# LayerNorm normalisations on VectorE: one scalar_tensor_tensor with a broadcast 1/std in place of tensor_scalar

## What is computed

```python
def _layernorm(x, axis=-1, eps=1e-05):
    m = jnp.mean(x, axis=axis, keepdims=True)
    v = jnp.var(x, axis=axis, keepdims=True)
    return (x - m) / jnp.sqrt(v + eps)

x = x + tanh(g_xattn[0]) * attn0(_layernorm(x), ctx)    # 16 heads of 64
x = x + tanh(g_ffn[0])   * moe0(_layernorm(x))          # 8 experts, thresholded softmax gate
x = x + tanh(g_xattn[1]) * attn1(_layernorm(x), ctx)    # 16 heads of 16
x = x + tanh(g_ffn[1])   * moe1(_layernorm(x))          # routed experts, first 512 rows only
```

## Time and profile before

| | |
|---|---|
| median of 3 runs | 3775.74 us (3772.87 to 3776.51) |
| the profiled execution, its own time | 3774.71 us |
| its span, first to last instruction | 3772.6 us |
| TensorE clock granted, mean | 0.996 of full |
| TensorE busy | 3665.2 us, 97% |
| VectorE busy | 2636.4 us, 70% |
| ScalarE busy | 1711.5 us, 45% |
| GpSimd busy | 1386.7 us, 37% |

### The profile page before, as it was taken

How to read it: one execution, slowest core, us unless ns; L and a number is a source line. 1 busy time by engine, 2 the same in 40 slices (tenths; PEclk the granted TensorE clock), 3 DMA queues, 4 the chain that set the end, 5 groups by cost and what they waited for, 6 DMA issues and landing times.

```text
span 3772.6 us, 95482 instructions
## 1 busy us (share of the span) xinstructions
PE 3665.2 (97%) x34836; PEld 2991.3 (79%) x34836; DVE 2636.4 (70%) x5694; ACT 1711.5 (45%) x3115; POOL 1386.7 (37%) x1333
## 2 busy tenths in 40 slices
PE   7999999999999999999999999999999999999998
PEld 5778878878878878878878878878878878878865
DVE  4676776776776776776776776776776776776775
ACT  4444444444444444444444444444444444444431
POOL 3333433433433433433433433433433433433323
PEclk9999999999999999999999999999999999999999
DMA  3000000000000000000000000000000000000001
GB/s 96 11 14 16 12 12 16 12 12 16 12 12 16 12 12 16 12 13 16 12 13 16 11 13 16 12 13 16 12 13 16 11 13 16 11 13 16 11 26 65
DMA packets 58916, 64.83 MB, mean 17 GB/s; under 512 B 5344, under 2 KB 55808, under 8 KB 58240
## 3 DMA queue, kind: packets, MB, share of 16 engines
q10 hardware_dynamic: 34688, 32.52, 2.8%
q1 hardware_dynamic: 24192, 31.81, 2.6%
HBM read 47.01 MB, written 17.30 MB: 17 GB/s over the span
## 4 chain that ended last, share of the span: by engine, by line
PE 91%; DVE 6%; ACT 1%; issue 1%; POOL 0%; SPq 0%; DMA 0%; DVEq 0%; ACTq 0%; POOLq 0%
PE g L818 28%; PE g L824 17%; PE scores L818 12%; PE scores L921 6%; PE g L971 6%; DVE xn L1177 4%; PE g L887 4%; PE g L990 3%; PE scores L955 3%; PE scores L981 3%; PE g L838 3%; PE scores L925 2%; PE g L898 1%; DVE kT_lo L1207 1%; ACT kT_hi L663 1%
## 5 line engine op out<-in xcount | busy, mean ns | idle before, releaser
L761 ACT ACTIVATE prob<-scores 120x1024 f32<-120x1024 f32 x512 | 498.5, 1023 | 509.0 <-PE scores L925 438.4
L1316 DVE SCALAR_TENSOR_TENSOR x<-g,lg_w,x 128x256 f32<-128x256 f32 x1024 | 494.8, 483 | 250.3 <-PE g L818 226.7
L597 POOL TENSOR_TENSOR q_lo<-an,q_hi 128x512 fp32r<-128x512 f32 x256 | 331.7, 1308 | 278.0 <-ACT q_hi L790 278.0
L818 PE MATMUL g<-ew_hi,yT_hi 128*128 128x512 f32 x1024 | 426.5, 416 | 0.0
L818 PE MATMUL g<-ew_lo,yT_hi 128*128 128x512 f32 x1024 | 401.7, 392 | 0.0
L818 PE MATMUL g<-ew_hi,yT_lo 128*128 128x512 f32 x1024 | 399.5, 390 | 0.0
L1255 DVE TENSOR_REDUCE y_nm<-g 128x4 f32<-128x480 f32 x512 | 301.0, 650 | 110.6 <-PE g L898 110.6
L542 POOL TENSOR_TENSOR y_rstd<-y_mv,eps 128x2 f32<-128x2 f32 x128 | 25.0, 195 | 960.7 <-DVE y_mv L1172 960.7
L1255 DVE TENSOR_REDUCE x_nm<-g 128x4 f32<-128x480 f32 x512 | 313.1, 654 | 82.6 <-PE g L887 82.6
L592 POOL TENSOR_TENSOR q_lo<-q_full,q_hi 128x512 fp32r<-128x512 f32 x256 | 330.3, 1299 | 65.3 <-ACT q_full L695 65.3
L542 POOL TENSOR_TENSOR x_rstd<-x_mv,eps 128x2 f32<-128x2 f32 x64 | 12.5, 195 | 886.1 <-DVE x_mv L1172 886.1
(11 more groups left out here) (213 smaller groups left out, 9540.8 us busy)
## 6 DMA issues: line engine op xcount, KB each, us to landing
x_in<-in_x ACTq DMA_DIRECT2D x64, 256.0 KB, 2.8
out<-y_x SPq DMA_DIRECT2D x64, 256.0 KB, 2.1
ctx_in<-in_ctx ACTq DMA_DIRECT2D x128, 120.0 KB, 2.3
wk_s<-in_gu SPq DMA_DIRECT2D x8, 512.0 KB, 3.4
vx<-in_ew SPq DMA_DIRECT2D x2, 1024.0 KB, 5.0
wk_s<-in_wk SPq DMA_DIRECT2D x1, 1024.0 KB, 5.2
prob<-in_wq SPq DMA_DIRECT2D x1, 1024.0 KB, 7.7
wv_s<-in_wv SPq DMA_DIRECT2D x1, 1024.0 KB, 10.4
```

What stands on the lines that cost most here:

```text
L597: g.tensor_tensor(q[1][:, 2 * h:2 * h + 2, :], an[:, 2 * (h % 2):2 * (h % 2) + 2, :], q[0][:, 2 * h:2 * h + 2, :].bitcast(F32), ALU.subtra ...
L761: a.activation(prob[:, e].rearrange("p o u s -> p (o u s)"), scores[0:NK, banks, :].rearrange("p o c -> p (o c)"), ACT.Exp, scale=scale).t ...
L818: ins = t_.matmul(out_, lhsT[u], rhs[v], start=first and n == 1, stop=last and n == 3 * len(terms))
L1316: ins = v.scalar_tensor_tensor(out=x1[:, t, :], in0=ring.bank(Y_FFN[j])[:, o * D:(o + 1) * D], scalar=lg_w[:, t, 2 * n + o:2 * n + o + 1], ...
```

## The change

In `normalise` the two per-partition scalars (mean, 1/std) were both pointer scalars of one tensor_scalar. Now the mean is the pointer scalar of a scalar_tensor_tensor, and 1/std is its second tensor: one SBUF column repeated over the 256 columns. The arithmetic (subtract, then multiply) and the number of instructions are the same; no instruction changes its place on any engine, and no wait is added or removed. m_norm (line 1354), in the last stage, keeps its tensor_scalar.

```diff
             def normalise(src, mv, rs, dst, normed):
                 for t in range(T):
-                    ins = v.tensor_scalar(dst[:, t, :], src[:, t, :], mv[:, t, 0:1], rs[:, 1, t:t + 1],
-                                          ALU.subtract, ALU.mult)
+                    ins = v.scalar_tensor_tensor(out=dst[:, t, :], in0=src[:, t, :], scalar=mv[:, t, 0:1],
+                                                 in1=rs[:, 1, t:t + 1].broadcast_to([P, D]),
+                                                 op0=ALU.subtract, op1=ALU.mult)
                 ins.then_inc(normed.sem, 1)
```

## The result

| | before | after |
|---|---|---|
| median | 3774.3 us (3769.06 to 3776.51, 4 runs) | 3802.97 us (3802.12 to 3803.61, 4 runs) |
| the profiled execution, its own time | 3774.71 us | 3802.79 us |
| its span | 3772.6 us | 3800.7 us |
| one turn of the loop (mean distance of n_norm's starts over 55 turns) | 56.60 us | 57.08 us |

The changed kernel is slower, ratio 1.0077, 95% interval 1.0065 to 1.0089. Forecast were 3808 us and a range of 3777 to 3822.

A forecast was written before the change was run, and what follows sets the result against it. TensorE, busy 97% of the span, bounds the kernel; VectorE counts only where TensorE waits for it. p_norm 16.1 + y_norm3 12.4 = 28.5 us (upper 40.9), taken as 33: 3774.7 + 33 = 3807.7, 3808 us; range 3777 to 3822.

The forecast's parts named there:

- The hold stays: At p_norm and y_norm3, the new two-tensor instruction still stands until the GpSimd instruction that came first is over.
- Rival A: Repeated column not read like a tensor, so no hold at p_norm and y_norm3; 55 us faster, 3720 us, chance 0.10.
- rival B: At p_norm the second xn gets in ahead of kmx, pair ends after 1.0 us; about 3730 us, chance 0.04.
- +0.13 behind a GpSimd instruction, up to 0.18: A held xn ends 0.28 us after GpSimd's instruction instead of 0.15 to 0.16, possibly 0.05 later still.
- the lower sum: p_norm's 16.1 us plus y_norm3's 12.4 us, 28.5 us in all; with the upper prices 40.9 us.
- p_norm, 2 x 0.13 in a turn: Both xn of p_norm end 0.13 us later, kmx moved on between: 0.26 a pair, 62 pairs, 16.1 us.
- y_norm3, 0.07 + 0.13: At y_norm3 first xn 0.07 us longer, moving q_lo on, second 0.13: 0.20 a pair, 62 pairs, 12.4 us.
- Rival C: Only p_norm counts; y_norm3's delay is avoided or partly taken up: 16 us remain, 3791 us, chance 0.14.
- n_norm at nothing: n_norm's pair grows from 0.73 to some 0.87 us, covered by VectorE's 0.15 us wait for TensorE; otherwise 9 us more.
- Nothing is given back: TensorE has no idle time behind p_norm and y_norm3 to give back any of the delay.
- rival D: The loss is absorbed, as the next turn's waits might depend on VectorE's queue: 3774 to 3782 us, chance 0.10.
- The signs named ahead: Profile after: xn<-x about 1160 ns, xn<-x_in some 475, TensorE's line 838 wait some 63 us, turn 57.1 us.

The follow-up runs named there:

- p_only: Kernel before with scalar_tensor_tensor only in p_norm's two instructions; y_norm3 and n_norm keep tensor_scalar: 3787.84 us, ratio 1.0043.
- y_only: Kernel before with scalar_tensor_tensor only in y_norm3's two instructions: 3784.43 us, ratio 1.0033.
- n_only: Kernel before with scalar_tensor_tensor only in n_norm's two instructions: 3772.43 us, ratio 1.0002.
- accum: Kernel before with tensor_scalar in all three normalisations also writing an accumulator to an unread scratch column allocated behind xn: 3715.98 us, ratio 0.9849.
- ts_order: Kernel before, tensor_scalar kept, p_norm moved ahead of kT_lo on VectorE and GpSimd's first q_lo of a batch waiting for it: 3717.27 us, ratio 0.9849.
- accum_py_last: Kernel before with accumulating tensor_scalar in p_norm and y_norm3, scratch column allocated behind all other SBUF tensors: 3706.66 us, ratio 0.9821.
- accum_y_last: Kernel before with accumulating tensor_scalar only in y_norm3, scratch column allocated behind all other SBUF tensors: 3766.7 us, ratio 0.9977.
- accum_y: Kernel before with accumulating tensor_scalar only in y_norm3, scratch column allocated right behind xn: 3774.32 us, ratio 1.0002.

## Why the prediction was right, point by point

- **The hold stays.** Right. It rested on rows of another instruction, tensor_tensor (y_an, ew_lo, w_lo). The kernel after shows it of scalar_tensor_tensor, in 188 instructions of 256: 0.28 to 0.29 behind GpSimd's end. Rival A, the repeated column that doesn't count as a tensor, falls with that; rival B too, as kmx still comes in ahead of the second xn.
- **+0.13 behind a GpSimd instruction, up to 0.18.** The lower price is the right one: 0.28 or 0.29 against 0.15 or 0.16. The 0.05 us that scalar_tensor_tensor has over tensor_tensor when alone does not show behind the hold. Here is nearly the whole error of the forecast: I took 33 us between the lower sum, 28.5, and the upper, 40.9; the medians lie 28.7 apart. The price rested on a single row, y_an's.
- **p_norm, 2 x 0.13 in a turn.** Right: +0.26 in p_only. That kmx is moved on by the first xn shows in its 1.97 for 1.83 us.
- **y_norm3, 0.07 + 0.13.** Right: +0.20 in y_only. Rival C, that it has slack, falls; the 0.12 us between xn's end and the weight load, the same as at p_norm, was the sign that it had none, although no wait was named.
- **n_norm at nothing.** Right: ratio 1.0002 with the longer form there alone. Its cover, 0.15 us for 0.14, held: n_only's VectorE waits 9.2 us less for TensorE.
- **Nothing is given back (rival D falls).** Right: TensorE's busy time is unchanged and the span grew by the sum.
- **The signs named ahead.** xn<-x at 1147 ns (1160 foreseen), xn<-x_in at 480 (475), a turn of 57.08 (57.1). TensorE's named wait for xn rose to 80.1 us instead of 63: y_norm3's waits, now 0.28 us long, are named too, some 18 us, as y_only shows.
- **What rival A would have given** was put at 55 us: 44.6 at p_norm and 5 to 15 at y_norm3. The hold can be removed, by another form or by order, and that gives 56 to 57 us (accum, ts_order), and 67.8 where both places are freed and no tensor is moved (accum_py_last). The size was wrong at p_norm: y_norm3 alone gives 7.8 us (accum_y_last), inside what was put down for it, but p_norm gives 57 (ts_order) to 60 us (67.8 less 7.8) in place of 44.6. For p_norm the prediction counted only TensorE's idle time, 0.72 us; the turn became 0.90 (ts_order) to 0.91 us (accum_py_last against accum_y_last) shorter.

## What to carry to other kernels

Before a VectorE instruction is replaced, see what holds it up: one whose duration spreads from 0.40 to 1.87 us for the same shape is not slow, it waits; here its end lay a fixed distance behind another engine's instruction. Then the form must be chosen by what it shares with that engine and not by its own length: the form that was 30% longer when alone (533 against 408 ns) made the kernel 1.8% faster, and the one with a second SBUF tensor, 18% longer and still held, 0.8% slower. A change of form also needs a look at what else it allocates, and a wait's worth is not read off its idle time alone: 0.72 us of it were worth 0.90 here.

## What the runs showed that was not expected

- A scratch tensor of eight bytes a partition in the middle of SBUF's layout, which moved the tensors behind it by 32, cost 9.3 us (ratio 1.0025), as much as a third of the change itself, and hid the whole gain of another edit in accum_y. A scratch tensor of an experiment belongs behind all others.
- Idle time is not all that an unready operand costs. At y_norm3 TensorE stood idle 0.07 us, and the profile named no wait, yet freeing it gave 0.13 us a turn (56.60 to 56.47), since the weight load also regains its lead over the matmuls. At p_norm 0.72 us were named and 0.90 gained.
